# Far key blocks with the table's last row added to the keys, and the program written out for 24 tiles, in a one-core attention and expert block

## The chip, the cores and the metric

One NeuronCore of a Trainium2 chip runs the whole program. The metric is the device time of one execution in microseconds, the median of several runs. All five engines run their own instruction streams and meet at semaphores: TensorE (PE; PEld is its weight load), VectorE (DVE), ScalarE (ACT), GpSimd (POOL), and SyncE (SP), which here only issues DMAs. Groups of matmuls write PSUM banks of 128 partitions x 512 numbers.

## The reference

x has 16 batches of 1024 positions and 256 channels. It is a layer of attention and a layer of low-rank experts, each between two layer norms and a residual sum:

```python
x = x + layernorm(attention(layernorm(x)))
x = x + layernorm(experts(layernorm(x)))
# attention, 16 heads of 16 channels, MAX_LEN = 512:
idx = r[None, :] - r[:, None] + (MAX_LEN - 1)        # key position minus query position
rel = rel_emb[idx]                                   # table of 1023 rows
qk = einsum('bhld,bhrd->bhlr', q, k) / sqrt(16) + einsum('bhld,lrd->bhlr', q, rel)
out = lin(einsum('bhlr,bhrd->bhld', softmax(qk), v), Wo, bo)
# experts: base product + shared low rank product + the best 2 of 6 routed low rank products
```

Positions reach 1024 and the table has 1023 rows, so an index goes from -512 to 1534. One above 1022 reads the table's last row: a key 512 or more positions ahead of the query always meets the same row. A negative index counts from the end of the table.

## The kernel before

**Tiles.** The program goes over NT = 128 query tiles t of 128 positions, eight (TPB) to a batch; `it` is the tile's number in its batch, b the batch. Each tile meets all 1024 keys of its batch, in NJP = 4 pairs jp of key blocks of 128 (c = 0, 1 within the pair) and NI = 4 query slices i of 32, so a tile has 16 groups g = 4 jp + i. A group's scores fill two PSUM banks (c = 0, 1) for 16 heads x 32 queries; three such pairs rotate (`buffer`). f32 operands are split into two f16 parts: the keys and queries lie in 96 rows as three products of the parts, for two heads.

**One group on TensorE** (`tile` at line 872): `scores(g, 0)`, then the transposes of the previous group's maxima (line 738), `scores(g, 1)`, `wide`, `mixed`, and `shift` (line 747), which subtracts the previous group's maximum from its scores. `scores` (lines 717 to 733) issues for one half 8 products of keys and queries (line 724) and then 12 products with the rel table (line 730): tw, a window of the table in 128 rows, against rm, masked copies of the queries. `wide` does the product of probabilities and values for the pair of key blocks before (line 757, in i = 1 and 2), its transposes in i = 3, and at i = 0 the projections of a later tile. `mixed` does the experts' products and others in the bank of the transposed maxima; before it, TensorE waits until VectorE has read that bank (`maxima_read`, line 785).

**The other engines.** VectorE takes per group the transposing maximum over both banks (line 1185), then side work of the tile (layer norms, routing; `side`, line 1200), then from the transposes the smaller reduction (line 1194) and the mask product nmm (line 1197), which `shift` needs. ScalarE takes the exponential (line 1018) behind `shift`, and copies PSUM to SBUF. POOL makes rm (line 592), splits f32 in two f16 parts (lines 605 and 607) and adds biases. All take their order from the program text; `passes` (line 317) puts tiles 0 and 1 ahead of a loop (`Fori`, line 320) over tiles 2 to 127 in bodies of UNROLL = 6 tiles, so the loop's back edge is taken 20 times: at tiles 8, 14, 20 and so on to 122.

**Projections and loads.** During tile t of batch b the queries, keys and values of the tile eight further on (batch b + 1) are computed; POOL's `split` at line 652 gives qkh and qkl, and SP stores them in DRAM (line 451) and the values at line 465. SP's order for a tile is written out in `tile` (lines 398 to 473). In it: wait for the tile's start, window of the rel table for the last pair of blocks (line 359); in a batch's first tile (`new`) the keys of the last pair, six loads (line 383); wait for the masks; six loads of the next tile's queries (line 375) and 24 for rm's source raw (line 366); the row of x for the residual (line 421); in a batch's first tile the values of the last pair (line 389); then windows 0, 1, 2 of the next tile, in the last tile of a batch with keys and values 0, 1, 2 of the next batch, between them the next x tile and the stores; last the result (line 472), for which it waits. SP's own loop runs over batches 1 to 13; batches 14 and 15 are written out. ScalarE issues a few loads at the start. The first batch's projections are made in a prologue.

Of the kernel before, what the change touches and what calls it, by code (L numbers as in the profile page):

```python
# [8 lines left out]
B, L, D = 16, 1024, 256  # L9
# [26 lines left out]
UNROLL = 2 * NBUF  # L36
# [8 lines left out]
def sandwich_kernel(nc, x, wqT, bq, wkT, bk, wvT, bv, woT, bo, relT, baseT, base_b,  # L45
# [7 lines left out]
    qk_s = nc.dram_tensor("qk_s", (2, 2, B + 1, D, L), f16, kind="Internal").ap()  # L53
    v_s = nc.dram_tensor("v_s", ((B + 1) * TPB, P, H * 32), f32, kind="Internal").ap()
# [4 lines left out]
    with ctx:  # L59
# [41 lines left out]
        ks = sb("ks", [ROWS, H // 2, L], f16)  # L101
        vs = sb("vs", [P, JC, H, 32])
# [105 lines left out]
        s_vs = [sem(f"s_vs{j}") for j in range(NJP)]  # L208
        s_raw = sem("s_raw")
# [104 lines left out]

        assert (NT - 2) % UNROLL == 0

        def passes(eng, tile):
            tile(0, TPB, att=True, proj=True, a=False, b=False, ph=0)
            tile(1, TPB + 1, att=True, proj=True, a=True, b=False, ph=1)
            with nc.Fori(2, NT, UNROLL, engines=(eng.engine,), hint_back_edge=True) as t:  # L320
                for k in range(UNROLL):
                    tile(t + k, t + (k + TPB), att=True, proj=True, a=True, b=True, ph=2 + k)
            tile(NT, None, att=False, proj=False, a=True, b=True, ph=NT % UNROLL)
            tile(NT + 1, None, att=False, proj=False, a=False, b=True)
# [3 lines left out]
        def _(sp):  # L328
# [56 lines left out]

            def load_values(b, jp):
                n = b * TPB + 2 * jp
                src = v_s[n:n + 2] if isinstance(n, int) else v_s[bass.ds(n, 2)]
                sp.dma_start(vs[:, 2 * jp:2 * jp + 2, :, :].rearrange("p c h d -> p c (h d)"),
                             src.rearrange("c p f -> p c f")).then_inc(s_vs[jp], 16)  # L390
# [7 lines left out]
            def tile(b, it, att, proj, a, bb, new=False, last=False, end=False, wrap=False, first=False):  # L398
# [24 lines left out]
                if new:  # L423
                    after(s_pv, t * NJP)
                    after(s_vst, n * 16)
                    load_values(b, NJP - 1)
                if att and not end:
                    nit = 0 if last else it + 1
                    after(s_scores, t * NG + NI)
                    load_window(nit, 0)  # L430
                    if last:
                        load_keys(b + 1, 0)
# [13 lines left out]
                if proj:  # L446
                    after(s_qks, t + 1)
                    for part, src in ((0, qkh), (1, qkl)):
                        for sel in range(2):
                            dst = qk_s[part, sel, b + 1].rearrange("(c p) t -> p c t", p=P)  # L450
                            sp.dma_start(dst[:, :, it * P:it * P + P] if isinstance(it, int)
                                         else dst[:, :, bass.ds(it * P, P)],
                                         src[:, 2 * sel:2 * sel + 2, :]).then_inc(s_qkst, 16)
                if last and not end:
                    after(s_pv, t * NJP + 2)
                    load_values(b + 1, 1)
# [18 lines left out]
            def first_stores(k):  # L475
# [4 lines left out]
                for part, src in ((0, first_h[k % 2]), (1, first_l[k % 2])):  # L480
                    for sel in range(2):
                        sp.dma_start(qk_s[part, sel, 0].rearrange("(c p) t -> p c t", p=P)[:, :, k * P:(k + 1) * P],
                                     src[:, 2 * sel:2 * sel + 2, :]).then_inc(s_qkst, 16)
                sp.wait_ge(s_vvp, k + 1)
# [17 lines left out]
            for jp in range(1, NJP):  # L502
                load_keys(0, jp)
                load_values(0, jp)
            tile(0, 0, True, True, False, False, first=True)
# [23 lines left out]
            sp.wait_ge(s_qkst, (NT + TPB) * 64)  # L529
            sp.wait_ge(s_vst, (NT + TPB) * 16)  # L530
# [3 lines left out]
        def _(pool):  # L534
# [73 lines left out]

            def ones_like(x):
                return one[0:x.shape[0], :].to_broadcast(tuple(x.shape))  # L610
# [4 lines left out]
            def tile(t, n, att, proj, a, b, ph=None):  # L615
# [30 lines left out]
                if proj:  # L646
# [5 lines left out]
                    split([flat(qkh[:, :, :]), flat(qkl[:, :, :])], flat(qkb[:, :, :]), s_qks)  # L652
                if a:
# [47 lines left out]
            for k in range(TPB):  # L701
# [5 lines left out]
                if k > 1:  # L707
                    pool.wait_ge(s_qkst, (k - 1) * 64)
                split([flat(first_h[k % 2][:, :, :]), flat(first_l[k % 2][:, :, :])], flat(qkb[:, :, :]), s_qksp)
# [4 lines left out]
        def _(pe):  # L714
            mm = nc.tensor.matmul

            def scores(g, c, buf, qb):

                jp, i = divmod(g, NI)
                bank = sc[:, 2 * buf + c, :]  # L720
                out3 = bank.rearrange("p (h i) -> p h i", i=IW)
                j = (2 * jp + c) * P
                for h in range(H // 2):
                    last = mm(bank[:, 2 * h * IW:(2 * h + 2) * IW], ks[:, h, j:j + P],  # L724
                              qm[:, qb, 2 * h:2 * h + 2, i * IW:(i + 1) * IW],
                              start=(h == 0), stop=False, skip_group_check=True)
                for m in range(IW // OCT):
# [144 lines left out]
            def tile(t, n, att, proj, a, b, ph=None):  # L872
                read = None
                for g in range(NG):
                    jp, k = divmod(g, NI)
                    old = a if g == 0 else att
                    if att:
# [3 lines left out]
                        if g == 0:  # L881
                            pe.wait_ge(s_qm, t * 96 + 96)
                        if jp == 0:
# [4 lines left out]
                        scores(g, 0, buffer(ph, g), ph % 2)  # L888
# [4 lines left out]
                    if att:  # L893
                        scores(g, 1, buffer(ph, g), ph % 2).then_inc(s_scores, 1)
# [48 lines left out]
        def _(act):  # L943
# [24 lines left out]
            assert N_CONST2 == 16 * 12  # L968

# [355 lines left out]
```

## Time and profile before

| | us |
|---|---|
| median of 3 runs | 6021.76 (6007.79 to 6028.19) |
| the profiled execution | 6024.29 |
| its span, first to last instruction | 6022.5 |
| TensorE busy (matmul; weight loads) | 5838.6; 5413.1 |
| VectorE, ScalarE, POOL busy | 4888.2; 3068.6; 3324.3 |
| mean granted clock of TensorE | 0.989 |
| DMA | 589.69 MB, mean 98 GB/s |

Busy times say which engines are close to full, but matmuls are pipelined, and a busy TensorE may still be one that could issue more. The starts of one VectorE instruction that comes once per group (line 1185) are a ruler: sixteen of them are a tile. What decides in a group is read from who waits for whom around it. The granted clock is 1.00 at TensorE's upper level, 2.4 GHz, and 0.50 at its lower, 1.2 GHz.

### The profile page before, as it was taken

How to read it: one execution, taken by the hardware profiler on the slowest of the kernel's cores; microseconds unless marked ns; L12 is line 12 of the kernel's file. 1: busy time of each engine (PE TensorE's matmuls, PEld its weight loads, DVE VectorE, ACT ScalarE, POOL GpSimd, SP SyncE). 2: the span in 40 equal slices, each digit the busy share in tenths (PEclk: the TensorE clock that was granted, in tenths of full speed). 3: DMA queues.
4: the chain of work that ended last, by engine and by line, in shares of the span. 5: the costliest groups of instructions: out<-in, count | busy, mean ns of one | idle time of the engine just before them, and what ended most of it. 6: DMA issues, size and time to landing. Idle time of an engine off the chain costs nothing.

```text
span 6022.5 us, 378834 instructions
## 1 busy us (share of the span) xinstructions
PE 5838.6 (97%) x161792; PEld 5413.1 (90%) x161792; DVE 4888.2 (81%) x10178; ACT 3068.6 (51%) x5160; POOL 3324.3 (55%) x5182
## 2 busy tenths in 40 slices
PE   6999999999999999999999999999999999999997
PEld 6999999999898999989999999999999989999896
DVE  5888888888787888888888888888888888888886
ACT  3555555555555555555555555555555555555554
POOL 4555555555555555555555555555555555555555
PEclk8999999999999999999999999999999999999998
DMA  6343343433434334343343434334343343433432
GB/s 148 87 104 93 93 109 85 107 98 85 110 91 104 95 86 114 93 106 88 90 116 84 113 93 97 97 92 113 85 105 98 90 109 90 113 88 87 113 90 55
DMA packets 1461077, 589.69 MB, mean 98 GB/s; under 512 B 1127168, under 2 KB 1425136, under 8 KB 1459376
## 3 DMA queue, kind: packets, MB, share of 16 engines
q1 hardware_dynamic: 1454752, 562.48, 37.6%
q8 instruction: 1303, 21.35, 1.6%
q14 instruction: 398, 3.26, 0.2%
q10 hardware_dynamic: 4624, 2.60, 0.2%
HBM read 476.43 MB, written 89.85 MB: 94 GB/s over the span
## 4 chain that ended last, share of the span: by engine, by line
PE 81%; DVE 9%; issue 4%; POOL 2%; DVEq 2%; POOLq 1%; SPq 0%; ACT 0%; DMA 0%
PE sc L730 21%; PE pw L757 15%; PE sc L747 14%; PE sc L724 14%; PE pm L778 4%; PE pw L778 4%; DVE r L1185 4%; PE pm L738 4%; PE pw L764 3%; DVE xn L1099 1%; DVEq L1196 1%; POOL rm L592 1%; DVE nmm L1197 1%; DVE y2n L1099 1%; PE pm L797 1%
## 5 line engine op out<-in xcount | busy, mean ns | idle before, releaser
L1185 DVE TRANSPOSE_TENSOR_REDUCE r<-sc 128x32 f16<-128x1024 f32 x2048 | 2544.2, 1242 | 19.7 <-PE sc L730 18.8
L1018 ACT ACTIVATE prob<-sc 128x1024 f32<-128x1024 f32 x2048 | 2098.0, 1024 | 210.0 <-PE sc L747 170.9
L730 PE MATMUL sc<-rm,tw 128*128 128x48 f16 (+1 forms) x49152 | 2154.2, 195 | 7.8 <-issue 7.4
L730 PEld LDWEIGHTS sc<-rm,tw 128*128 128x128 f16 x49152 | 1763.6, 100 | 9.8 <-issue 9.4
L724 PE MATMUL sc<-qm,ks 96*128 96x64 f16 x32768 | 1643.9, 193 | 60.6 <-POOL rm L592 43.2
L724 PEld LDWEIGHTS sc<-qm,ks 96*128 96x128 f16 x32768 | 1305.7, 98 | 71.9 <-issue 42.4
L1194 DVE TENSOR_REDUCE nm<-pm 16x32 f16<-16x256 f32 x2048 | 835.3, 408 | 627.5 <-PE pm L738 609.1
L747 PE MATMUL sc<-nmm,pick 128*128 128x64 f16 x32768 | 1302.9, 194 | 32.7 <-DVE nmm L1197 24.3
L747 PEld LDWEIGHTS sc<-nmm,pick 128*128 128x128 f16 x32768 | 1135.1, 98 | 172.2 <-DVE nmm L1197 81.1
L757 PE MATMUL pw<-prob,vs 128*32 128x128 f32 x32768 | 1117.1, 276 | 12.1 <-issue 6.2
L757 PEld LDWEIGHTS pw<-prob,vs 128*32 128x32 f32 x32768 | 840.0, 110 | 74.8 <-issue 13.8
L592 POOL TENSOR_TENSOR rm<-raw,mask_r 128x192 f16<-128x192 f16 (+1 forms) x1545 | 887.3, 604 | 20.7 <-PE sc L730 11.4
L1197 DVE TENSOR_TENSOR nmm<-nm,mask_h 16x64 f16<-16x64 f16 x2048 | 630.4, 308 | 189.3
L738 PE MATMUL pm<-ident,r 128*128 128x128 f16 x4096 | 573.3, 222 | 1.7 <-issue 1.1
L947 ACT ACTIVATE ot<-pw 128x512 f32<-128x512 f32 x512 | 304.8, 595 | 482.7 <-PE pw L757 482.7
L605 POOL TENSOR_TENSOR oT<-oT,one 128x256 f16<-128x256 f32 x128 | 78.4, 612 | 762.1 <-ACT oT L947 762.1
L947 ACT ACTIVATE nmt<-pm 128x16 f32<-128x16 f32 x512 | 93.7, 183 | 758.7 <-PE pm L797 758.7
L634 POOL TENSOR_TENSOR wp<-parts,wst 128x1088 f32<-128x1088 f32 x128 | 262.5, 2051 | 181.8 <-ACT parts L947 181.8
L599 POOL TENSOR_TENSOR ve<-mv,eps 128x1 f32<-128x1 f32 x513 | 113.3, 221 | 408.1 <-DVE mv L1096 408.1
L764 PE MATMUL pw<-ident,ot 128*128 128x128 f32 x2048 | 325.1, 281 | 0.7 <-ACT ot L947 0.7
L601 POOL TENSOR_TENSOR rs<-ve,mhalf 128x1 f32<-128x1 f32 x513 | 281.6, 549 | 75.4 <-issue 2.7
L605 POOL TENSOR_TENSOR hT<-hT,one 112x128 f16<-112x128 f32 x128 | 51.2, 400 | 490.6 <-ACT hT L947 490.6
(153 smaller groups left out, 5780.8 us busy)
## 6 DMA issues: line engine op xcount, KB each, us to landing
raw<-qk_s SPq DMA_DIRECT2D x3096, 64.0 KB, 2.9
tw<-tw_s SPq DMA_DIRECT2D x512, 288.0 KB, 3.9
v_s<-vpad SPq DMA_DIRECT2D x136, 256.0 KB, 3.3
vs<-v_s SPq DMA_DIRECT2D x64, 512.0 KB, 4.3
qm<-qk_s SPq DMA_DIRECT2D x768, 32.0 KB, 2.1
ks<-qk_s SPq DMA_DIRECT2D x378, 64.0 KB, 3.4
qk_s<-qkh SPq DMA_DIRECT2D x272, 64.0 KB, 2.8
qk_s<-qkl SPq DMA_DIRECT2D x272, 64.0 KB, 2.7
```

The lines of the kernel that those rows point to most:

```text
L592: last = g.tensor_tensor(rm[:, i, :, c * H:(c + n) * H].rearrange("p m (h e) -> p m h e", e=n), src[:, :, :, q:q + n], mask_r[:, c:c + n]. ...
L724: last = mm(bank[:, 2 * h * IW:(2 * h + 2) * IW], ks[:, h, j:j + P], qm[:, qb, 2 * h:2 * h + 2, i * IW:(i + 1) * IW], start=(h == 0), stop ...
L730: last = mm(out3[:, :, OCT * m + q:OCT * m + q + n], tw[:, s, jp, u:u + P], rm[:, i, m, r * H:(r + n) * H].rearrange("p (h e) -> p h e", e=n),
L738: last = mm(p_max[:, c * P:(c + 1) * P], r1[:, c * H:c * H + P], ident16[:, :], start=True, stop=True)
L747: last = mm(pairs[:, :, h, :], pick[:, h, :], nmm[:, :, :], start=False, stop=True, skip_group_check=True)
L757: last = mm(pw[32 * q:32 * q + 32, col * P:(col + 1) * P], vs[:, 2 * jp + c, h, :], prob[:, jp % 2, c, h, :], start=(c == 0), stop=(c == 1))
L764: last = nc.tensor.transpose(pw[:, col * P:(col + 1) * P], ot[:, col, :], ident[:, :])
L778: last = mm(dst, lhs, rhs, start=(m == 0), stop=(m == len(steps) - 1))
L1018: A(prob[:, jp % 2, :, :, i * IW:(i + 1) * IW], sc[:, 2 * buf:2 * buf + 2, :].rearrange("p c (h i) -> p c h i", i=IW), ACT.Exp).then_inc(s ...
L1185: v.tensor_reduce(r1[:, 0:2 * H], sc[:, 2 * buf:2 * buf + 2, :].rearrange("p c (h i) -> p (c h) i", i=IW), axis=AX.X, op=ALU.max, apply_tr ...
L1194: v.tensor_reduce(part, p_max[0:H, :].rearrange("h (q i) -> h i q", i=IW), axis=AX.X, op=ALU.max, negate=True).then_inc(s_nmr, 1)
L1197: v.tensor_tensor(nmm[0:H, :, :], part.rearrange("h (a i) -> h a i", a=1) .to_broadcast((H, 2, IW)), mask_h[:, :, :], ALU.mult).then_inc(s ...
```

## The change

Key block j = 2 jp + c is far if j - it >= FAR = 5: all its keys are then at least 513 positions ahead of all queries of the tile, and the rel row is the table's last. For those blocks the 12 rel products of a half group are left out, and the keys come from kf, which holds key + last row of the table (as two f16 parts, in the layout of ks) for the last three blocks of a batch (NF = 3). POOL computes it (`far_keys`) behind the split of the projections of tiles 5, 6 and 7, from the f32 keys qkb; SP stores it in DRAM (`store_far`) and loads it in six DMAs (`load_far`) in the first tile of the batch that uses it, behind the values of the last pair. TensorE waits for it before group 8 of that tile. ScalarE loads rfar, the last row, eight times, once for each 16 partitions. The loop's body has UNROLL = TPB * NBUF = 24 tiles, in 5 turns; tiles 122 to 127 are written out behind it.

```diff
-UNROLL = 2 * NBUF
+UNROLL = TPB * NBUF
+TURNS = (NT - 2) // UNROLL
+FAR = MAX_LEN // P + 1
+NF = TPB - FAR
...
+        kf = sb("kf", [ROWS, H // 2, NF * P], f16)
...
-            with nc.Fori(2, NT, UNROLL, engines=(eng.engine,), hint_back_edge=True) as t:
+            with nc.Fori(2, 2 + TURNS * UNROLL, UNROLL, engines=(eng.engine,), hint_back_edge=True) as t:
                 for k in range(UNROLL):
                     tile(t + k, t + (k + TPB), att=True, proj=True, a=True, b=True, ph=2 + k)
+            for t in range(2 + TURNS * UNROLL, NT):
+                tile(t, t + TPB, att=True, proj=True, a=True, b=True, ph=t)
...
+            def store_far(b, it):
+                for part, src in ((0, kfh), (1, kfl)):
+                    dst = kf_s[part, b].rearrange("(c p) t -> p c t", p=P)
+                    sp.dma_start(dst[:, :, (it - FAR) * P:(it - FAR + 1) * P], src[:, :, :]).then_inc(s_kfst, 16)
+            def load_far(b):
+                for s in range(2):
+                    for k, part in enumerate(SPLIT_ST):
+                        r = (3 * s + k) * HD
+                        src = kf_s[part, b].rearrange("(h s d) t -> s d h t", s=2, d=HD)
+                        sp.dma_start(kf[r:r + HD, :, :], src[s, :, :, :]).then_inc(s_kf, 16)
...
                     load_values(b, NJP - 1)
+                    after(s_kfst, b * (32 * NF) + 32 * NF)
+                    load_far(b)
...
+                    if it >= FAR:
+                        after(s_kfs, b * NF + (NF + it - FAR + 1))
+                        store_far(b + 1, it)
...
+            def far_keys(stored):
+                if stored is not None:
+                    pool.wait_ge(s_kfst, stored)
+                g.tensor_tensor(flat(kfb[:, :, :]), flat(qkb[:, 2:4, :]), rfar[:, :].to_broadcast((P, 2 * P)), ALU.add)
+                pool.drain()
+                split([flat(kfh[:, :, :]), flat(kfl[:, :, :])], flat(kfb[:, :, :]), s_kfs)
...
                     split([flat(qkh[:, :, :]), flat(qkl[:, :, :])], flat(qkb[:, :, :]), s_qks)
+                    if ph % TPB >= FAR:
+                        far_keys(batch_of(t) * (32 * NF) + 32 * (NF + ph % TPB - FAR))
...
                 for h in range(H // 2):
-                    last = mm(bank[:, 2 * h * IW:(2 * h + 2) * IW], ks[:, h, j:j + P],
+                    keys = kf[:, h, j - FAR * P:j - FAR * P + P] if far else ks[:, h, j:j + P]
+                    last = mm(bank[:, 2 * h * IW:(2 * h + 2) * IW], keys,
...
+                if far:
+                    return last
...
+                        if ph % TPB == 0 and g == FAR // 2 * NI:
+                            pe.wait_ge(s_kf, batch_of(t) * 96 + 96)
...
+            for k in range(TPB):
+                act.dma_start(rfar[k * HD:(k + 1) * HD, :], relT[:, NREL - 1:NREL],
+                              allow_slow_non_contiguous=True).then_inc(s_rfar, 16)
```

The prologue gets the same pieces: far_keys for the first batch's tiles 5 to 7, their stores, and load_far(0) ahead of the loads of keys and values 2 and 3.

## Rows read from the trace of the kernel before

**Rows 1.** The page's part 4: shares of the chain that ended last, by engine

```profile
PE 81%; DVE 9%; issue 4%; POOL 2%; DVEq 2%; POOLq 1%; SPq 0%; ACT 0%; DMA 0%
```

**Rows 2.** Timeline of VectorE (start us, us, engine line, operation): maxima of tiles' group 0

```profile
675.60 1.23 DVE L1185 TRANSPOSE_TENSOR_REDUCE r<-sc 128x32 f16<-128x1024 f32 x1
...
770.23 1.23 DVE L1185 TRANSPOSE_TENSOR_REDUCE r<-sc 128x32 f16<-128x1024 f32 x1
...
3122.39 1.23 DVE L1185 TRANSPOSE_TENSOR_REDUCE r<-sc 128x32 f16<-128x1024 f32 x1
...
3167.63 1.23 DVE L1185 TRANSPOSE_TENSOR_REDUCE r<-sc 128x32 f16<-128x1024 f32 x1
...
5653.02 1.23 DVE L1185 TRANSPOSE_TENSOR_REDUCE r<-sc 128x32 f16<-128x1024 f32 x1
...
5746.98 1.23 DVE L1185 TRANSPOSE_TENSOR_REDUCE r<-sc 128x32 f16<-128x1024 f32 x1
```

**Rows 3.** Timeline of VectorE: maxima of groups 8, 9 and 15 of tile 66

```profile
3144.83 1.25 DVE L1185 TRANSPOSE_TENSOR_REDUCE r<-sc 128x32 f16<-128x1024 f32 x1
...
3147.09 1.24 DVE L1185 TRANSPOSE_TENSOR_REDUCE r<-sc 128x32 f16<-128x1024 f32 x1
...
3164.67 1.25 DVE L1185 TRANSPOSE_TENSOR_REDUCE r<-sc 128x32 f16<-128x1024 f32 x1
```

**Rows 4.** Timeline of TensorE: the 12 rel products of a half group, what follows

```profile
3148.70 0.52 PE L730 MATMUL sc<-rm,tw 128*128 128x48 f16 x12
3149.05 0.28 PE L738 MATMUL pm<-ident,r 128*128 128x128 f16 x2
```

**Rows 5.** Timelines of ScalarE and TensorE: exponential of group 11, values' product in 13

```profile
3157.42 1.02 ACT L1018 ACTIVATE prob<-sc 128x1024 f32<-128x1024 f32 x1
...
3158.61 1.08 PE L757 MATMUL pw<-prob,vs 128*32 128x128 f32 x32
```

**Rows 6.** A back edge (timeline, window with clock), and the loop's end (timeline)

```profile
3212.68 0.29 PEld L724 LDWEIGHTS sc<-qm,ks 96*128 96x128 f16 x8 [2.07 <-ACT prob L1018]
...
3214.70:3218.10 3.40, 3.40 (x70) 3.29 (x72) 1.74 (x3) 1.68 (x3) 3.26 (x7) 0.67 0.46 145
...
5973.57 0.29 PE L738 MATMUL pm<-ident,r 128*128 128x128 f16 x2 [0.54 <-DVE r L1185]
```

**Rows 7.** Timelines of SP and TensorE, first tiles of batches 1, 8 and 15

```profile
468.79 0.40 PE L724 MATMUL sc<-qm,ks 96*128 96x64 f16 x8
...
473.14 0.40 SPq L389 DMA_DIRECT2D vs<-v_s  x1
...
3036.24 4.17 SPq L383 DMA_DIRECT2D ks<-qk_s  x6
...
3044.52 15.51 SPq L366 DMA_DIRECT2D raw<-qk_s  x24
...
3051.56 0.40 PE L724 MATMUL sc<-qm,ks 96*128 96x64 f16 x8
...
3062.51 0.39 SPq L389 DMA_DIRECT2D vs<-v_s  x1
...
5628.17 0.40 PE L724 MATMUL sc<-qm,ks 96*128 96x64 f16 x8
...
5631.06 0.39 SPq L389 DMA_DIRECT2D vs<-v_s  x1
```

**Rows 8.** One line's instructions, L383, six loads of a pair's keys: issue to landing

```profile
DMA to landing us min/median/max: 2.2/3.4/7.0
```

**Rows 9.** Windows: us, busy PE, PEld, DVE, ACT, POOL (x), PEclk, DMA share, GB/s

```profile
86.90:90.20 3.30, 3.05 (x50) 3.08 (x51) 1.10 (x3) 0.00 (x0) 0.00 (x0) 0.51 1.24 215
```

**Rows 10.** Timelines of POOL and VectorE, tile 67: qkl and a mask product

```profile
3183.88 1.16 POOL L607 TENSOR_TENSOR qkl<-qkb,qkh 128x512 f16<-128x512 f32 x1
...
3184.41 0.67 DVE L1197 TENSOR_TENSOR nmm<-nm,mask_h 16x64 f16<-16x64 f16 x1
```

**Rows 11.** Waits of SP's queue: us in total, times, longest

```profile
SPq L396 <- POOL res L695: 1703.4, 128, 26.3
```

More of the change, by code:

```diff
@@ L53, in sandwich_kernel @@
     qk_s = nc.dram_tensor("qk_s", (2, 2, B + 1, D, L), f16, kind="Internal").ap()
+    kf_s = nc.dram_tensor("kf_s", (2, B + 1, D, NF * P), f16, kind="Internal").ap()
     v_s = nc.dram_tensor("v_s", ((B + 1) * TPB, P, H * 32), f32, kind="Internal").ap()
@@ L101, in sandwich_kernel @@
         ks = sb("ks", [ROWS, H // 2, L], f16)
+        kf = sb("kf", [ROWS, H // 2, NF * P], f16)
+        rfar = sb("rfar", [P, 1])
+        kfb = sb("kfb", [P, 2, P])
+        kfh = sb("kfh", [P, 2, P], f16)
+        kfl = sb("kfl", [P, 2, P], f16)
         vs = sb("vs", [P, JC, H, 32])
@@ L208, in sandwich_kernel @@
         s_vs = [sem(f"s_vs{j}") for j in range(NJP)]
+        s_rfar = sem("s_rfar")
+        s_kfs = sem("s_kfs")
+        s_kfst = sem("s_kfst")
+        s_kf = sem("s_kf")
         s_raw = sem("s_raw")
@@ L305, in batch_of @@
             return t // TPB
-        assert (NT - 2) % UNROLL == 0
         def passes(eng, tile):
@@ L483, in first_stores @@
                                      src[:, 2 * sel:2 * sel + 2, :]).then_inc(s_qkst, 16)
+                if k >= FAR:
+                    sp.wait_ge(s_kfs, k - FAR + 1)
+                    store_far(0, k)
                 sp.wait_ge(s_vvp, k + 1)
@@ L504, in _ @@
                 load_values(0, jp)
+                if jp == 1:
+                    sp.wait_ge(s_kfst, 32 * NF)
+                    load_far(0)
             tile(0, 0, True, True, False, False, first=True)
@@ L529, in _ @@
             sp.wait_ge(s_qkst, (NT + TPB) * 64)
+            sp.wait_ge(s_kfst, (B + 1) * 32 * NF)
             sp.wait_ge(s_vst, (NT + TPB) * 16)
@@ L708, in _ @@
                     pool.wait_ge(s_qkst, (k - 1) * 64)
+                if k >= FAR:
+                    if k == FAR:
+                        pool.wait_ge(s_rfar, 16 * TPB)
+                    far_keys(32 * (k - FAR) if k > FAR else None)
                 split([flat(first_h[k % 2][:, :, :]), flat(first_l[k % 2][:, :, :])], flat(qkb[:, :, :]), s_qksp)
@@ L715, in _, with scores @@
             mm = nc.tensor.matmul
-            def scores(g, c, buf, qb):
+            def scores(g, c, buf, ph):
                 jp, i = divmod(g, NI)
+                it, qb = ph % TPB, ph % 2
+                far = 2 * jp + c - it >= FAR
                 bank = sc[:, 2 * buf + c, :]
@@ L887, in tile @@
                             pe.wait_ge(s_exp, free)
-                        scores(g, 0, buffer(ph, g), ph % 2)
+                        scores(g, 0, buffer(ph, g), ph)
                     if read is not None:
@@ L893, in tile @@
                     if att:
-                        scores(g, 1, buffer(ph, g), ph % 2).then_inc(s_scores, 1)
+                        scores(g, 1, buffer(ph, g), ph).then_inc(s_scores, 1)
                     wide(t, n, g, att, proj, a)
```

## The prediction

> **What bounds the kernel now.** I read the chain that ended last first: TensorE carries 81% of it and VectorE 9% [rows 1]. Then I looked at one tile of 128 queries. VectorE's transposing maximum (line 1185) runs once per group, sixteen times a tile, and its starts are the clock of the kernel: an undisturbed tile takes 3167.63 - 3122.39 = 45.24 us [rows 2]. TensorE is without a gap in most of it, but not everywhere. Two groups show the other limit. From group 8 to group 9 the maxima follow each other in 3147.09 - 3144.83 = 2.26 us, and from group 15 to the next tile's group 0 in 3167.63 - 3164.67 = 2.96 us [rows 2, 3]. In both TensorE had its products ready and VectorE's own loop decides (maximum, TensorE's two transposes of it, the small reduction, the mask product, next maximum; in groups 14 and 15 there are normalisations between them). So 2.26 us is the floor of a group, whatever is taken off TensorE, and groups 14, 15 and the next tile's 0 are VectorE's.
>
> **Part 1: far blocks lose their rel products.** A key block is far if it is five or more ahead: three blocks at query tile 0 of a batch, two at tile 1, one at tile 2, six of 64. Each has four groups, so 24 half groups a batch lose 12 products each. In the trace the twelve start at 3148.70 and the transposes behind them at 3149.05: 0.35 us for one half group [rows 4]. That is 24 x 0.35 = 8.4 us a batch and 134 us in 16 batches, the upper end. How much of it survives is worked out by group, from the tile of rows 2 and 3:
> - Tile 0, groups 8 to 11, only the second half is relieved. Group 8 to 9 is at the floor already. 9 to 10 falls from 2.89 to about 2.71: the product with the values waits for the exponential of two groups earlier, which takes 1.02 us. 10 to 11 falls from 3.03 to 2.69. 11 to 12, where both halves of group 12 are relieved, falls from 2.89 to the floor, 2.3.
> - Group 12 to 13: 2.84 to 2.50, because the product with w_base shares its bank with the transposed maxima and waits until the small reduction has read them. Group 13 to 14: only 2.91 to 2.82. The exponential of group 11 ends at 3158.44 and TensorE's product with the values starts at 3158.61 [rows 5]: that wait is 0.17 us away now, and 0.7 us taken off TensorE runs into it.
> - Groups 14 and 15: nothing, VectorE's loop.
> Tile 0 gains 0.18 + 0.34 + 0.59 + 0.34 + 0.09 = 1.5 us, tile 1 (groups 12 to 15 only, one floor step of 0.24) 0.7 us, tile 2 (one half only) 0.2 us: 2.4 us a batch, **-38 us**. Bounds: 0 and -134; I take 38 since each limit named stands within 0.2 us of TensorE in the rows.
>
> **Part 2: the loop over 24 tiles instead of 6.** At a back edge TensorE stands still: at tile 68 its weight load waits 2.07 us, and in the 3.4 us behind the products run at a granted clock of 0.67 [rows 6], part of them at 1.2 GHz. The pair of tiles around an edge takes, for the first edge that is not also a change of batch, 770.23 - 675.60 = 94.63 us, for the last 5746.98 - 5653.02 = 93.96 [rows 2], against 2 x 45.24 = 90.48. There are 15 such edges; their excess lies between 1.4 and 4.2 us, 3.1 in the mean. 20 edges are taken before, 4 after. Leaving the loop costs nothing: behind the last pass TensorE's next step stands idle for 0.54 us, and for VectorE's maximum, not for its program [rows 6]. 16 x 3.1 = **-50 us**. Bounds: 16 x 1.4 = 22 and 16 x 4.2 = 67. The longer program is not fetched again and again (a loop body of 6 tiles isn't kept either, as the edges show), so I take no cost for it.
>
> **Part 3: the new load and where it stands in SP's queue.** Here the change adds its largest term. load_far(b) is issued in tile 0 of batch b itself, behind load_values(b, 3); TensorE waits for it before group 8 of the same tile (before the scores, with all that is queued behind them). SP's queue at a batch's first tile, batch 8 [rows 7]: six key loads from 3036.24, six query loads, 24 raw loads from 3044.52 for 15.51 us, the x row, and the values at 3062.51. TensorE starts group 8's scores at 3051.56. So the place where the new loads go comes 10.95 us after they are needed. The same distance is 473.14 - 468.79 = 4.35 us at the first of the 15 changes of batch and 5631.06 - 5628.17 = 2.89 at the last [rows 7]. Between them it is near 9.5 us, but in five (the first is one) a TensorE back edge falls on the same tile and holds TensorE up by 3 to 4 us: this cover goes with part 2. So I take 9.5 for the 13 in SP's loop, and 6.6 and 2.9 for the two written out. To that comes: 0.6 us to the next issue, 3 us until the sixth is issued (six key loads take 4.17 us in rows 7, from the first issue to the end of the last), 3.4 us for the last to land, the median of the key loads [rows 8]: 7.0 us. Stall: 13 x 16.5 + 13.6 + 9.9 = **+238 us**. Bounds: with the shortest and the longest landing of a key load, 2.2 and 7.0 us [rows 8], the 7 us become 5.8 to 10.6, so 15 x (-1.2 to +3.6): 220 to 292. I take the median, since each of the six moves 96 KB against 64 KB of a key load, but in pieces half as long again.
>
> **After each stall the clock.** After a pause of TensorE in the prologue the granted clock is 0.51 from 86.90 to 90.20, which is the 1.2 GHz level, with 50 matmuls in 3.30 us [rows 9], where an undisturbed tile issues the 12 of rows 4 in 0.35 us. At half speed 3.3 us of products lose 1.6 us; if the level comes back only after twice that, 3.3: 2.2 us a stall taken, nearer to the row: 15 x 2.2 = **+33 us**. The Trainium skill, "TensorE: Matmul & The Clock Gate", section "HAM oscillation", warns of exactly this, waits on a DMA between bursts of matmuls, and by it each of the 15 stalls ends on the lower level; the row agrees for one.
>
> **Part 4: far_keys on POOL** (query tiles 5, 6, 7). Three more steps of 128x256 behind the split of q and k, each about half of the 1.16 us of qkl, which is 128x512 [rows 10]. POOL then waits for other engines anyway, so the time itself is hidden. But POOL's steps hold up VectorE: the 16x64 mask product that starts at 3184.41 under qkl takes 0.67 us and ends at 3185.08, with qkl (3183.88 + 1.16 = 3185.04) [rows 10]. The last of the new steps would end near 3187.4, over the start of the next mask product: 0.2 us in 48 tiles, **+10 us**; bounds 0 and 48 x 0.6 = 29. The Trainium skill, "SBUF — State Buffer", section "SBUF: two separate sides", says the pair of ports shared by the two engines is locked for a whole instruction; by that alone each new step could cost its whole length once, the upper bound here; the row agrees in kind (0.67 us, ending with qkl).
> SP's two more stores on those tiles and its wait for far_keys are hidden: SP waits 1703.4 us in all, in 128 times, for the tile's result at its end [rows 11]. Queued behind the new wait are the next windows, values and keys; if that cover were gone, the stall of part 3 would grow by the 1 to 2 us of it.
>
> **Part 5: the prologue.** Three times far_keys, three pairs of stores, eight tiny loads on ACT's queue and six loads ahead of the keys 2 and 3: most beside other loads, **+6 us**, bounds 0 and 15.
>
> **Sum.** 6024.3 us (the profiled execution; its span is 6022.5) - 38 - 50 + 238 + 33 + 10 + 6 = 6223 us. The median of the runs shown is 2.5 us below the profiled one: 6221 us, 3.3% slower.
>
> **Rivals.**
> - *The stall is hidden (ends faster).* If SP reached the new loads 7 us before TensorE needs them, only the other terms stay: 6024 - 38 - 50 + 10 + 6 - 2.5 = 5950 us. The place is SP's queue in a batch's tile 0, the price 15 times the lateness, and it turns at a values load 7 us ahead of group 8's scores; the rows show it 2.9 to 11 us behind. 4%.
> - *The edges give nothing back*: their cost is that of fetching the program and comes wherever 6 tiles end. For: single gaps of 0.3 to 1 us in the middle of the loop body. Against: leaving the loop is free. 6271 us, 13%.
> - *The far blocks give nothing*: VectorE's loop and the exponential take it all. 6259 us, 13%.
> - *The far loads land late*: 96 KB in small pieces behind 512 KB of values, 11 us or more instead of 7, or a cold TensorE for longer. 6285 us and more, 8%.
> - The main case: 62%.
> That the change doesn't do what it says (the wait already met because the count is reached early) I exclude: the count of batch b is only complete with the sixth load of that batch.
>
> **Range and chances.** The main case with its bounds runs from about 6165 (stalls 220, clock 24, edges 67, the rest at its lower ends) to 6290 (stalls 292, clock 50); the second and third rival lie inside, the fourth partly: 6160 to 6290. A difference of 0.3% is what a measurement of this kernel tells from none. Faster by more 4%, within 1%, slower 95%.
>
> **What would show it.** A wait of TensorE on a DMA into kf, 15 times, 10 to 19 us, on the line of the first scores of group 8; none in batch 0. In SP's queue six kf issues behind the values load. Far tiles otherwise: tiles 1 of a batch 0.7 us shorter. Pairs of tiles at the edges gone at all but four places. The small mask product longer on tiles 5 to 7. It is wrong if kf's wait is short or absent, or if tiles without far blocks change length.

## The result and the profile after

| | us |
|---|---|
| before, median of 4 runs | 6023.68 (6007.79 to 6028.19) |
| after, median of 4 runs | 6200.11 (6191.13 to 6207.33) |
| ratio | 1.0297, 95% interval 1.0274 to 1.0320 |
| span of the profiled execution after | 6189.3 (its time 6191.13) |

The change makes the kernel 176 us slower; the terms of the forecast add up to 199. The page after, its parts 4 and 5 (chain by engine and by line; then groups of instructions: busy us, mean ns, idle time before them and what ended it):

```profile
PE 72%; DVE 9%; SPq 7%; issue 5%; POOL 2%; DVEq 2%; DMA 1%; ACT 1%; POOLq 1%
...
L780 PE MATMUL sc<-qm,ks 96*128 96x64 f16 x29696 | 1487.2, 193 | 281.4 <-DMA kf<-kf_s 256.2
...
L805 PE MATMUL sc<-nmm,pick 128*128 128x64 f16 x32768 | 1304.5, 193 | 77.4 <-DVE nmm L1260 66.6
```

In the chain of before SP's queue had no share and TensorE 81% [rows 1]; now SP's queue has 7% of it, and DMA, kf's landing in the main, another 1%. The line of the key products (724 before, 780 now) stands idle for 256.2 us, waiting for the loads into kf. The waits of TensorE (us in total, times, longest):

```profile
PE sc L780 <- DMA kf<-kf_s: 256.2, 15, 18.9
```

Fifteen waits of 17.1 us in the mean, none in batch 0. This is one of them, with SP's queue and TensorE at the first tile of batch 8, the tile of the middle [rows 7] (line numbers have moved: the maximum is line 1248, the values' load 416, kf's load 411):

```profile
3128.27 13.10 SPq L380 DMA_DIRECT2D raw<-qk_s  x24
3141.71 0.36 SPq L448 DMA_DIRECT2D xr<-x  x1
3142.49 0.39 SPq L416 DMA_DIRECT2D vs<-v_s  x1
3143.22 2.79 SPq L411 DMA_DIRECT2D kf<-kf_s  x6
```

```profile
3134.69 1.25 DVE L1248 TRANSPOSE_TENSOR_REDUCE r<-sc 128x32 f16<-128x1024 f32 x1
...
3134.84 0.63 PE L805 MATMUL sc<-nmm,pick 128*128 128x64 f16 x16
3151.22 0.59 PE L780 MATMUL sc<-qm,ks 96*128 96x64 f16 x8 [15.75 <-DMA kf<-kf_s]
...
3153.32 1.25 DVE L1248 TRANSPOSE_TENSOR_REDUCE r<-sc 128x32 f16<-128x1024 f32 x1
...
3157.58 1.25 DVE L1248 TRANSPOSE_TENSOR_REDUCE r<-sc 128x32 f16<-128x1024 f32 x1
```

TensorE is done with group 7 at 3135.5 and stands idle from there, the values are issued at 3142.49, the six loads of kf from 3143.22, and group 8's first product runs at 3151.22. Group 7 to 8 takes 3153.32 - 3134.69 = 18.63 us in place of 2.75, and the next group 4.26 in place of 2.26. Why that one too, the windows of the same stretch tell (us, busy time and count of PE, PEld, DVE, ACT, POOL, then PEclk, DMA share, GB/s):

```profile
3137.00:3145.00 8.00, 0.00 (x0) 0.00 (x0) 0.00 (x0) 0.00 (x0) 0.00 (x0) 0.70 0.59 143
3145.00:3148.00 3.00, 0.00 (x0) 0.00 (x0) 0.00 (x0) 0.00 (x0) 0.00 (x0) 0.50 1.12 225
...
3151.50:3155.00 3.50, 3.50 (x44) 3.13 (x42) 2.03 (x5) 0.55 (x2) 0.00 (x0) 0.50 0.46 111
3155.00:3158.50 3.50, 3.50 (x82) 3.21 (x80) 1.50 (x4) 1.24 (x2) 1.97 (x3) 0.67 0.02 5
3158.50:3162.00 3.50, 3.50 (x113) 3.24 (x110) 2.73 (x7) 2.00 (x5) 0.40 (x1) 1.00 0.00 0
```

While TensorE has nothing to do its granted clock falls to 0.50, 1.2 GHz, and stays there in the first windows of work: 44 matmuls in 3.5 us against 113 once it is back.

The gains of the change are in the same trace. First maxima of tiles 65, 66 and 67:

```profile
3176.58 1.23 DVE L1248 TRANSPOSE_TENSOR_REDUCE r<-sc 128x32 f16<-128x1024 f32 x1
...
3220.49 1.23 DVE L1248 TRANSPOSE_TENSOR_REDUCE r<-sc 128x32 f16<-128x1024 f32 x1
...
3265.86 1.23 DVE L1248 TRANSPOSE_TENSOR_REDUCE r<-sc 128x32 f16<-128x1024 f32 x1
```

Tile 65, the second of its batch, takes 43.91 us against 45.24 for an undisturbed tile [rows 2]; 44.55 is its median over the batches. Tile 66, with one far block, takes 45.37.

I add up the two profiled executions by the starts of the 2048 maxima, 166.8 us apart in time. Groups 7 to 8 of the 15 first tiles: +258.7. The groups behind them: +24.7. Up to the first maximum of tile 1: 139.92 - 126.08 = +13.8. First tiles otherwise: -37.5. All other tiles from 1 to 126: from 86.2 us over 45.25 each to 5.5 under, -91.7. The last tile and what follows it: -1.2. Sum +166.8.

### The profile page after: what moved, and what is told of

Same layout as the page of the kernel before. It is cut to its first block, busy times and chain, and to the rows that moved or that the text cites. A ratio compares the mean times of both kernels' runs of the same rounds, so it can differ in the third digit from the quotient of the medians.

```text
span 6189.3 us, 369723 instructions
## 1 busy us (share of the span) xinstructions
PE 5717.1 (92%) x157184; PEld 5280.7 (85%) x157184; DVE 4888.2 (79%) x10178; ACT 3068.9 (50%) x5160; POOL 3421.9 (55%) x5335
## 4 chain that ended last, share of the span: by engine, by line
PE 72%; DVE 9%; SPq 7%; issue 5%; POOL 2%; DVEq 2%; DMA 1%; ACT 1%; POOLq 1%
PE sc L788 17%; PE pw L815 13%; PE sc L805 13%; PE sc L780 12%; PE pm L836 4%; DVE r L1248 4%; PE pw L836 4%; PE pm L796 4%; SPq L380 3%; PE pw L822 3%; DMA kf<-kf_s 1%; POOL rm L631 1%; DVE nmm L1260 1%; DVEq L1259 1%; DVE xn L1162 1%
## 5 line engine op out<-in xcount | busy, mean ns | idle before, releaser
L788 PE MATMUL sc<-rm,tw 128*128 128x48 f16 (+1 forms) x44544 | 1949.4, 195 | 1.3 <-issue 1.2
L780 PE MATMUL sc<-qm,ks 96*128 96x64 f16 x29696 | 1487.2, 193 | 281.4 <-DMA kf<-kf_s 256.2
L788 PEld LDWEIGHTS sc<-rm,tw 128*128 128x128 f16 x44544 | 1596.2, 100 | 1.1 <-issue 1.0
L780 PEld LDWEIGHTS sc<-qm,ks 96*128 96x128 f16 x29696 | 1179.3, 98 | 293.2 <-issue 284.9
L805 PE MATMUL sc<-nmm,pick 128*128 128x64 f16 x32768 | 1304.5, 193 | 77.4 <-DVE nmm L1260 66.6
L1260 DVE TENSOR_TENSOR nmm<-nm,mask_h 16x64 f16<-16x64 f16 x2048 | 643.8, 314 | 196.1 <-issue 7.8
```

Source lines behind the costliest of these rows:

```text
L780: last = mm(bank[:, 2 * h * IW:(2 * h + 2) * IW], keys, qm[:, qb, 2 * h:2 * h + 2, i * IW:(i + 1) * IW], start=(h == 0), stop=False, skip_ ...
L788: last = mm(out3[:, :, OCT * m + q:OCT * m + q + n], tw[:, s, jp, u:u + P], rm[:, i, m, r * H:(r + n) * H].rearrange("p (h e) -> p h e", e=n),
L805: last = mm(pairs[:, :, h, :], pick[:, h, :], nmm[:, :, :], start=False, stop=True, skip_group_check=True)
L1260: v.tensor_tensor(nmm[0:H, :, :], part.rearrange("h (a i) -> h a i", a=1) .to_broadcast((H, 2, IW)), mask_h[:, :, :], ALU.mult).then_inc(s ...
```

## The experiments

Each was timed in turns with the kernel before, whose median was 6022.04 us beside early, later, loop24 and early_relkept, 6021.15 beside sumtwice, warm and early2, and 6017.75 beside tiny and warm2.

**early: the same loads, moved to the front of the same tile in SP's queue.** They go ahead of 38 issues: six of keys, six of queries, 24 of raw, the x row and the values (36 in the text on record).

```diff
                         if new:
+                            after(s_kfst, b * (32 * NF) + 32 * NF)
+                            load_far(b)
                             after(s_qkst, n * 64)
                             load_keys(b, NJP - 1)
...
                     load_values(b, NJP - 1)
-                    after(s_kfst, b * (32 * NF) + 32 * NF)
-                    load_far(b)
```

> The kernel after, with one move: load_far(b) is issued at the front of a batch's first tile, ahead of the six key loads, 36 issues earlier in SP's queue. Theory (lateness): the 15 waits for kf (256.2 us) and the slow groups behind them (24.7 us in group 8) go, nothing else changes: 6200 - 281 = about 5920 us, under the kernel before. Rival (the load itself or its store is slow, not its place): a wait of several us a batch stays, 5950 to 6100 us. Rival (moved cost): the 24 raw loads, the last keys and values land 3 us later and something waits for them: over 5950 us, with waits on raw, ks or vs in the first tiles.

Measured: 5933.44 us, ratio 0.9860 (0.9845 to 0.9876). No wait for kf is left in the trace. SP's queue in the same first tile:

```profile
2998.33 3.51 SPq L411 DMA_DIRECT2D kf<-kf_s  x6
3002.19 3.66 SPq L397 DMA_DIRECT2D ks<-qk_s  x6
3006.18 3.22 SPq L389 DMA_DIRECT2D qm<-qk_s  x6
3009.50 15.49 SPq L380 DMA_DIRECT2D raw<-qk_s  x24
```

TensorE reaches group 8's scores at 3009.95 and does not stop. One moved call takes 267 us off the kernel after and makes it 1.4% faster than the one before: the place was the whole loss. It is 17 us less than the 283.4 us of the stalls and slow groups in the trace. The traces place what was given back: against the kernel after, early's first tiles are 8.4 us longer outside those two groups, and the other tiles 16.8 us, half of that in the second tiles of the batches. Why is open. The raw loads moved back make no new wait: both traces have one on raw, of 7.5 us.

**later: the same loads, still further back.** load_far(b) moved from behind the values to behind the four stores of q and k of the same tile.

```diff
                     load_values(b, NJP - 1)
-                    after(s_kfst, b * (32 * NF) + 32 * NF)
-                    load_far(b)
...
+                    if new:
+                        after(s_kfst, b * (32 * NF) + 32 * NF)
+                        load_far(b)
                     if it >= FAR:
```

> The kernel after, with load_far(b) put further back in the same tile, behind the window, the x tile, a second window and the four stores of q and k, about 5.0 us later in SP's queue. Theory: each us of lateness is a us of TensorE's wait, 15 times, and the clock's price behind it does not grow: +75 us, 6275 us, waits for kf of 256 + 75 = 331 us. Rival (the price is that of stopping at all, of restart and clock): no more than 10 us on top, 6210 us.

Measured: 6233.32 us, ratio 1.0353 (1.0337 to 1.0370), 33 us above the kernel after; waits for kf 299.7 us in 15. Both expectations were off. In SP's queue

```profile
3159.97 0.39 SPq L416 DMA_DIRECT2D vs<-v_s  x1
...
3165.00 3.19 SPq L411 DMA_DIRECT2D kf<-kf_s  x6
```

the loads start 5.03 us behind the values in place of 0.73, so 4.3 us later. But they land sooner. From issue to landing (min/median/max), first the kernel after, then later:

```profile
DMA to landing us min/median/max: 4.0/4.8/8.5
```

```profile
DMA to landing us min/median/max: 2.8/3.3/8.3
```

In the kernel after, right behind the 512 KB of values, a load of kf takes 1.5 us longer than here, behind four stores of 64 KB. In early, where it stands behind a window of 288 KB, the median is 3.5. 15 x (4.3 - 1.5) = 42 us, and the waits grew by 43.5. So lateness is paid one for one, at its landing and not at its issue. The groups behind the stalls cost 26.0 us (24.7 in the kernel after): that price does not grow with the stall.

**loop24: the loop part alone,** in the kernel before.

```diff
-UNROLL = 2 * NBUF
+UNROLL = TPB * NBUF
+TURNS = (NT - 2) // UNROLL
...
-            with nc.Fori(2, NT, UNROLL, engines=(eng.engine,), hint_back_edge=True) as t:
+            with nc.Fori(2, 2 + TURNS * UNROLL, UNROLL, engines=(eng.engine,), hint_back_edge=True) as t:
...
+            for t in range(2 + TURNS * UNROLL, NT):
+                tile(t, t + TPB, att=True, proj=True, a=True, b=True, ph=t)
```

> The kernel before with the loop part of the change alone: bodies of 24 tiles and six tiles written out behind. Forecast on record: 16 back edges at 3.1 us, -50 us, 5973 us. Reading of the trace after: all tiles but a batch's first lose 92 us of excess over 45.25 us, 12 to 14 of them by far blocks, so -78 us, 5945 us. Rival (nothing saved by the loop, all by far blocks): 6023 us.

Measured: 5960.49 us, ratio 0.9896 (0.9880 to 0.9912): -62 us, between the two. The four edges that are left (tiles 26, 50, 74, 98) still cost 1.5, 2.4, 2.2 and 1.7 us against two undisturbed tiles; the exit at tile 122 costs 8.5. TensorE there:

```profile
5638.15 0.82 PE L732 MATMUL sc<-rm,tw 128*128 128x48 f16 x12 [3.36 <-issue]
```

It waits 3.36 us for nothing that the profile shows ("issue"), in the middle of group 0 of the first tile written out; that it waits for its program is the reading that is left, and no run tests it.

The traces also show what most of the old edges cost. In the kernel before, at 16 of the 20, TensorE stands before group 0 of the next tile until POOL's rm is there, 1.7 to 3.6 us each. The row at tile 68, and TensorE's waits for rm in the kernel before, then in loop24 (us in total, times, longest):

```profile
3212.69 0.40 PE L724 MATMUL sc<-qm,ks 96*128 96x64 f16 x8 [1.96 <-POOL rm L592]
```

```profile
PE sc L724 <- POOL rm L592: 43.2, 17, 7.7
```

```profile
PE sc L726 <- POOL rm L594: 10.3, 1, 10.3
```

The one wait that loop24 keeps, and the longest of before, lie ahead of tile 1. At the four edges that loop24 keeps TensorE stops for 0.58 to 0.64 us and not for rm. Why POOL is late at the edges of the short body alone, no run shows. The loop part's gain isn't all at the edges either: of the 60 us between the two profiled executions, 4.5 lie before the first maximum of tile 1.

**early_relkept: early, with ks and the rel products for the far half groups too.** kf is made, stored, loaded and waited for, and not used; the far products are computed as in the kernel before.

```diff
-                    keys = kf[:, h, j - FAR * P:j - FAR * P + P] if far else ks[:, h, j:j + P]
+                    keys = ks[:, h, j:j + P]
...
-                if far:
-                    return last
```

> As early, but the far half groups take ks and their 12 rel products as in the kernel before; kf is still computed, stored, loaded and waited for, and not used. Against early it gives the far products alone: forecast 38 us (2.4 us a batch); from the trace after 1.7 + 0.7 + 0.03 us a batch, 40 us. Against loop24 it gives the overhead of POOL, SP, DMA and prologue alone: forecast 10 + 6 us; from the trace 12 to 14 us, all of it in the prologue and tile 0, none on tiles 5 to 7.

Measured: 5970.56 us, ratio 0.9915 (0.9902 to 0.9929). Against early the far products are worth 37 us. Against loop24 everything that serves them costs 10 us. Each ratio's interval is 8 to 10 us to either side, so the 37 stand clear of it and the 10 do not. The four runs make a ladder from the kernel before: -62 for the loop (loop24), +10 for making and loading kf (early_relkept), -37 for the far products (early), +267 for the place of the load (the kernel after). It adds up to 178 us, where 176 were measured directly.

**sumtwice, then tiny: does far_keys on POOL hold up VectorE?** In the kernel after, tiles 5 to 7 take 45.27 us in the median, as tile 3 does (tile 4 takes 45.46). POOL's three steps and VectorE's instructions on tile 69:

```profile
3374.00 0.61 POOL L652 TENSOR_TENSOR kfb<-qkb,rfar 128x256 f32<-128x256 f32 x1
3374.76 0.61 POOL L644 TENSOR_TENSOR kfh<-kfb,one 128x256 f16<-128x256 f32 x1
3375.51 0.67 POOL L646 TENSOR_TENSOR kfl<-kfb,kfh 128x256 f16<-128x256 f32 x1
```

```profile
3375.34 0.17 DVE L1296 COPY best<-order 128x2 f32<-128x2 f32 x1
...
3376.22 0.18 DVE L1260 TENSOR_TENSOR nmm<-nm,mask_h 16x64 f16<-16x64 f16 x1
```

The last step ends at 3376.18 and the mask product starts at 3376.22; the gap is 0.03 to 0.04 us on all 48 tiles 5 to 7. sumtwice puts the first step twice:

```diff
                 g.tensor_tensor(flat(kfb[:, :, :]), flat(qkb[:, 2:4, :]), rfar[:, :].to_broadcast((P, 2 * P)), ALU.add)
                 pool.drain()
+                g.tensor_tensor(flat(kfb[:, :, :]), flat(qkb[:, 2:4, :]), rfar[:, :].to_broadcast((P, 2 * P)), ALU.add)
+                pool.drain()
```

> As early, with POOL's first step of far_keys (kfb, 0.61 us) done twice on each of the far_keys tiles. In the trace after, the last of the three steps ends at 3376.18 and VectorE's mask product of group 6 starts at 3376.22: it is missed by 0.04 us. Theory (a lock for a whole step, on a loop that is VectorE's there): one more step puts the last one over the mask product, 0.3 to 0.5 us a tile in 48 tiles, +15 to +24 us, 5950 us, and the tiles 5, 6 and 7 at 45.6 to 45.7 us. Rival (POOL's steps cost VectorE nothing there): 5933 us and 45.27 us a tile.

Measured: 5932.71 us, ratio 0.9854 (0.9839 to 0.9869), and tile 69 has the cycles of early. This was no test: the mask product, at 3234.62, fell into the gap between two POOL steps, 3234.52 to 3234.66. tiny shifts the steps by a third of a microsecond:

```diff
                 g.tensor_tensor(flat(kfb[:, :, :]), flat(qkb[:, 2:4, :]), rfar[:, :].to_broadcast((P, 2 * P)), ALU.add)
                 pool.drain()
+                g.tensor_tensor(scr[:, :], mhalf[:, :], eps[:, :], ALU.add)
+                pool.drain()
```

> As early, with one more 128x1 step and a drain between the first and the second step of far_keys, some 0.35 us. In sumtwice VectorE's mask product (3234.62) fell into the 0.14 us gap between two POOL steps, 3234.52 to 3234.66, so it was no test. Here the last step should lie over the mask product from 0.35 us before it to 0.3 us behind. Theory (lock for a whole step): mask product of group 6 on tiles 5 to 7 takes 0.4 to 0.5 us in place of 0.18, these tiles 45.5 us in place of 45.27, +12 us, 5945 us. Rival: 0.18 us, 45.27 us and 5933 us.

Measured: 5949.65 us, ratio 0.9881 (0.9864 to 0.9897), 16 us above early by the medians, 13 by the ratios, whose intervals overlap. So the tiles decide: 5 to 7 take 45.49 us in their median, 0.22 more, which is 11 us in 48 tiles. The rows of tile 69, POOL's and VectorE's:

```profile
3244.85 0.61 POOL L645 TENSOR_TENSOR kfh<-kfb,one 128x256 f16<-128x256 f32 x1
3245.61 0.68 POOL L647 TENSOR_TENSOR kfl<-kfb,kfh 128x256 f16<-128x256 f32 x1
```

```profile
3245.10 0.39 DVE L1299 COPY best<-order 128x2 f32<-128x2 f32 x1
...
3246.20 0.18 DVE L1263 TENSOR_TENSOR nmm<-nm,mask_h 16x64 f16<-16x64 f16 x1
```

The size was as expected, the instruction was not: the copy of two numbers, 0.17 us before, lasts 0.39 and ends with POOL's kfh (3245.46), and all behind it moves by 0.22. It is so on 47 of the tiles 5 to 7 and on no other tile. So on tiles 5 to 7 far_keys costs nothing in the kernel after by its timing alone, not because POOL has time.

**warm, then warm2: is the slow group the clock?** TensorE gets products to do while it waits, into the bank that group 8 then overwrites.

```diff
-                        if ph % TPB == 0 and g == FAR // 2 * NI:
-                            pe.wait_ge(s_kf, batch_of(t) * 96 + 96)
...
                             pe.wait_ge(s_exp, free)
+                        if ph % TPB == 0 and g == FAR // 2 * NI:
+                            if ph:
+                                for z in range(WARM):
+                                    mm(sc[:, 2 * buffer(ph, g), 0:2 * IW], ks[:, z % 8, 0:P],
+                                       qm[:, ph % 2, 0:2, 0:IW], start=True, stop=True)
+                            pe.wait_ge(s_kf, batch_of(t) * 96 + 96)
                         scores(g, 0, buffer(ph, g), ph)
```

> The kernel after, but in the 15 first tiles that stand still TensorE issues 520 extra products of keys and queries (some 15 us of them) into the bank that group 8 is about to overwrite, and only then waits for kf. The load comes as late as before, only the clock differs. Theory (group 8's 24.7 us behind the stalls are products at 1.2 GHz): they go, 6200 - 24 = 6176 us; group 8 to 9 back at 2.3 us from 4.07. Rival (they are the restart of the chain over four engines): group 8 stays near 4 us and the time at 6200 us.

Measured: 6236.11 us, ratio 1.0357 (1.0342 to 1.0372), and group 8 still at 4.07 us in the median: in 13 of the 15 the products ended 0.7 to 6.1 us before kf landed, so neither theory was tried there. In batch 8 it was 3.6 us, and the granted clock behind them was at 0.50 again. kf landed later too, and the stalls are 2.8 us longer: with TensorE at work SP takes 14.8 to 16.8 us to issue the 24 raw loads that stand ahead, against 12.9 to 14.3 in most stalls of the kernel after. Why it does is open.

> As warm, with 720 extra products (some 22 us) in place of 520, which ended 3.6 us before kf landed, so that TensorE works until after the landing. Theory (clock): TensorE stays at a granted clock of 1.00 through group 8 and group 8 to 9 takes 2.9 us, not 4.06 (2.26 is not reached, since VectorE has no side work to finish first). Rival (restart): 4.06 stays. The total says little: every stall is now as long as the 720 products, 22 us against 17, about +70 us on the kernel after less the clock's 17 to 24: 6250 us.

Measured, with 720 products: 6274.98 us, ratio 1.0424 (1.0406 to 1.0441). TensorE in batch 8:

```profile
3188.17 1.82 PE L950 MATMUL sc<-qm,ks 96*128 96x64 f16 x57 [0.70 <-issue]
3189.83 0.40 PE L781 MATMUL sc<-qm,ks 96*128 96x64 f16 x8
```

No gap, eight products of 96x64 in 0.40 us against 0.59 behind the stall in the kernel after, and group 8 to 9 takes 2.41 us. Over the 15 the excess of group 8 falls from 24.7 to 5.7 us. It stays at 4.07 in one, batch 6, and that one speaks for the clock too. kf had landed at 2417.87, before the products ended, but they have a stop of 2.35 us near their end, and the clock is down behind it. Its last extra products, the 3.5 us from their start, and 3.5 us of batch 8's group 8 (columns as above):

```profile
2420.41 0.42 PE L950 MATMUL sc<-qm,ks 96*128 96x64 f16 x9 [2.35 <-issue]
```

```profile
2420.40:2423.90 3.50, 3.49 (x48) 3.12 (x48) 1.78 (x3) 0.23 (x1) 0.00 (x0) 0.57 0.02 5
```

```profile
3189.80:3193.30 3.50, 3.42 (x91) 3.22 (x87) 2.30 (x6) 1.65 (x3) 0.79 (x2) 1.00 0.38 88
```

VectorE and ScalarE start again from nothing in all 15, and group 8 is slow only where the clock is low. The slow groups were the clock. The Trainium skill, "TensorE: Matmul & The Clock Gate", section "HAM oscillation", describes such waits on a DMA between bursts; the trace after agrees in all 15, at 0.9 to 2.0 us each, 1.65 in the mean.

**early2: early, with the prologue in another order.** POOL splits q and k ahead of the two splits of the far keys; SP stores the values first and loads kf behind keys and values 2.

```diff
+                    pool.drain()
+                    far_sum()
                 split([flat(first_h[k % 2][:, :, :]), flat(first_l[k % 2][:, :, :])], flat(qkb[:, :, :]), s_qksp)
+                if k >= FAR:
+                    far_keys(32 * (k - FAR) if k > FAR else None, summed=True)
...
-                if jp == 1:
+                if jp == 2:
                     sp.wait_ge(s_kfst, 32 * NF)
                     load_far(0)
```

> As early, with the prologue's order changed: POOL adds the row first, then splits q and k, then the far keys; SP stores the values ahead of the far keys and loads kf behind the keys and values 2. The prologue with tile 0 is 12 us longer in early than in the kernel before (4.8 us to the first maximum and 7.5 us in tile 0). Theory (late release of ACT's and SP's steps by far_keys on POOL, and the kf loads ahead of keys 2): 6 to 9 us of the 12 come back, 5926 us. Rival (it is DMA traffic or the longer program): 5933 us.

Measured: 5929.09 us, ratio 0.9842 (0.9828 to 0.9855). The first maximum of tile 1 (early, then early2):

```profile
138.41 1.23 DVE L1248 TRANSPOSE_TENSOR_REDUCE r<-sc 128x32 f16<-128x1024 f32 x1
```

```profile
131.96 1.23 DVE L1255 TRANSPOSE_TENSOR_REDUCE r<-sc 128x32 f16<-128x1024 f32 x1
```

It comes at 126.08 in the kernel before: of 12.3 us, 6.4 are back. In the medians it is 4 us, within the interval. By its median this is the fastest version run, 1.6% below the kernel before.

## Why the prediction was right

The time, 6200 us, lies inside 6160 to 6290 and 21 us under the forecast; the case that came is the one given 62%. The total is closer than its terms, and part of that is luck: stall and prologue cost more than was said, the loop gave more, clock and far_keys cost less, and these errors partly cancel.

| term | forecast | measured | by |
|---|---|---|---|
| far products | -38 | -37 | early against early_relkept |
| loop of 24 tiles | -50 | -62 | loop24 |
| stall for kf | +238 | +256 | waits in the trace after |
| clock behind the stalls | +33 | +25 | group 8; warm2 |
| far_keys beside VectorE | +10 | 0 | tiles 5 to 7 |
| prologue | +6 | +14 | first maximum of tile 1 |

The measured terms add up to 196 us and not to 176, since they are read in different places: the 256 and 25 don't count what the other tiles gave back beside the stalls. The ladder of the four runs leaves no such rest (178). The recorded range is uneven as well: its lower end moves every cost term, its upper end only stall and clock.

- **Part 1** held group by group: the limits that it named (exponential, bank of the maxima, VectorE's loop) decide, and not how much work leaves TensorE. In first tiles the steps 9 to 14 now take 2.66, 2.57, 2.24, 2.50 and 2.78 us where 2.71, 2.69, 2.3, 2.50 and 2.82 were said. What was missed: group 14 to 15 takes 3.11 us in place of 3.02 there. 134 us of products left TensorE by the row's price (its busy time fell by 121.5) and 37 reached the total; much of the rest became waits. TensorE's waits for the mask product rise from 24.3 us to 66.6 in all, those for the exponential from none to 19.0 and those for the reduction of the maxima from 0.8 to 12.5.
- **Part 2** had the sign and not the size. The step "leaving the loop costs nothing" failed: the exit cost 8.5 us in loop24 and 9.0 in early_relkept. I had read it at tile 128, where the written out end follows and VectorE is late anyway. In the kernel after itself it costs 1.2 us over two of 45.25, and TensorE has no such stop there. The mean of 3.1 us left out the five edges that are also a change of batch. Their pairs are 5.7 us over, where changes of batch without an edge are 1.5 over, so 4.1 us is the edge's. The remaining edges were to cost 3.1 us each and cost 1.5 to 2.4 in loop24, and 4.5 us came before tile 1. "TensorE stands still at an edge" was right, but mostly for POOL's rm, not for its own jump. In the kernel after the edges at tiles 50, 74 and 98 seem to cost nothing (two tiles take 0.0 to 0.5 us less than two of 45.25, such a pair without an edge 0.6 less). That is no rule of far blocks: with the same loop and far blocks these three cost 3.4 to 3.7 us each in early2, and the one at tile 98 costs 2.6 in early. What decides it is open.
- **Part 3** named the place, the count (15, none in batch 0) and the size. Its two halves erred against each other. From TensorE's last product to the values load 9.5 us were taken and 7.0 measured in the middle batch (8.1 in the mean of the 15, where 8.9 were taken); from there to group 8 it was 7.0 taken and 8.7 measured (9.0 in the mean). The term that was too small is the landing: 4.8 us in the median of all loads and 5.7 in the mean of the sixth, which ends the wait, where 3.4 was taken. The values right ahead, named by the fourth rival, fit it (the sixth lands in 3.3 in later). Issue took 2.8 us, where 3 was taken. The 9.9 us for the last batch were 14.7: there SP reached the values 4.8 us behind TensorE, not 2.9, and kf's loads were the slowest to land.
- **The clock** came at the lower end of its span: 1.65 us a stall, where 1.6 to 3.3 was the span and 2.2 taken.
- **Part 4** failed in its timing: the new steps follow one another faster than assumed (2.18 us for three), and the last one ends 0.04 us ahead of the product it was to hold up. That the lock exists and that 0.2 us a tile is its size, tiny shows. The Trainium skill, "SBUF — State Buffer", section "SBUF: two separate sides", gives the rule of one lock for a whole step. By its words each of the three steps could be paid in full, 1.9 us a tile; the bound of 0.6 counted one of them. Neither is reached: tiny pays 0.22, and a mask product that starts 0.09 us before a step's end is not held at all.
- **Part 5** was too small: 13.8 us up to tile 1 (12.3 in early, of which 6.4 come back by order alone in early2). Kernels with the same prologue spread over 3 us there.

Three rivals are out: no stall (early is what that kernel would be, 5933 us where 5950 was said), no gain from the loop (loop24), none from the far products (early_relkept). The fourth, loads that land 11 us or more behind the values' place instead of 7, was half right: it is 9.0 in the mean, and 9.9 in batches 14 and 15.

## What to carry to other kernels

A new load goes into the queue where it is needed, not where the code for its neighbour stands: count the issues ahead of it (here 38, at 0.4 to 0.7 us each for those in runs of six and 24) and compare with the moment of its wait. Read the cover of a gain before the gain: of work taken off the bounding engine here 28% came through, and most of the loss could be read beforehand, from VectorE's loop and from waits that stood 0.2 us away. Check such a sum by adding the changes one at a time as well: here the terms read one by one came to 196 us, the ladder of runs to 178. Where an added step on one engine seems free, shift it by a fraction of a microsecond before believing it.

## What the runs showed of the hardware that was not expected

- Six loads of 96 KB right behind one of 512 KB take 4.8 us from issue to landing, in the median, 3.3 behind four stores of 64 KB and 3.5 behind a window of 288 KB.
- Dense products in a stall save the clock only if they last until its end without a long stop. In batch 8 of warm they ended 3.6 us early and group 8 took 4.07 us, about as without them. In warm2, where they ran until kf was there, it took 2.41 with a stop of 0.70 us among them (batch 8) and 4.07 with one of 2.35 just before their end (batch 6).
- A written out tail behind a loop can cost more on entry (8.5 us in loop24, 3.36 of it one stop of TensorE) than any back edge of that program (2.4); in the kernel after it is 1.2 us.
- SP's issues take longer beside a working TensorE: 24 raw loads take 14.8 to 16.8 us to issue in the stalls of warm, and 12.9 to 14.3 in batches 2 to 13 of the kernel after, where TensorE stands idle. Why is open.
- A VectorE copy of two f32 numbers a partition is held up by a POOL step (0.39 us in place of 0.17, in tiny), while the 16x64 product that began 0.09 us before the end of another was not.
